# Linear attention in a perceiver block: each key-value and attention product issued as four products of 32 stationary columns on four column positions of TensorE

## The chip, the cores and the metric

The kernel runs on one core of one Trainium2 chip. The metric is the device time of one execution in microseconds (us); lower is better. A change of over 0.5% of it is about what a measurement of this kernel can tell from none.

## What is computed

The reference is one block of a perceiver on x (8 sequences of 64 rows, 512 wide) and a context (8 of 512 rows): cross attention, linear attention, and a mixture of 16 experts with a shared feed-forward, each behind a layernorm and added to x. The change lies in the linear attention alone:

```python
q_proj = _elu1(jnp.einsum('bhnd,hdf->bhnf', q, proj_matrix))   # 16 heads, hd 32, 128 features
k_proj = _elu1(jnp.einsum('bhnd,hdf->bhnf', k, proj_matrix))
kv = jnp.einsum('bhnf,bhnd->bhfd', k_proj, v)
attn = jnp.einsum('bhnf,bhfd->bhnd', q_proj, kv)
k_sum = k_proj.sum(axis=2)
z = 1.0 / (jnp.einsum('bhnf,bhf->bhn', q_proj, k_sum) + 1e-08)
attn = attn * z[..., None]
```

## The kernel before, in words

The 512 tokens (8 sequences of 64) are four tiles of 128 tokens, two sequences in each. Each engine has its own instruction stream, written out by hand, and semaphores tie them together. Cross attention comes first (to about 280 us), then a layernorm, the projection to q, k and v (`qkv_project`, L1127), the linear attention (339 to 388 us), the output product (`residual`, L1093), and the experts.

The order of the linear attention is one list, `LIN_ORDER` (L270 to L282), which PE (TensorE), ACT (ScalarE) and DVE (VectorE) all walk through. Its units are:

- "k" (L1147): the key features of four heads for one token tile, four matmuls with 128 stationary columns and 256 moving ones, in the f32r type. Each is one hardware matmul. ACT takes exp (L560) and for some units relu (L562) of the result, DVE puts them together as `k_feat` (L806, or L810 and L811).
- "q" (L1153): the query features of one head for all 512 tokens, two f32r matmuls with 512 moving columns; ACT and DVE as above (L560, L562, L806).
- "kv" (L1164): for one token tile and four heads, the product of `k_feat` (128 tokens by 128 features, stationary) with `v_bd` (128 tokens by 96 columns, moving: 2 sequences by 48, of which 32 are v and one is ones, for the sum of the features). These are full f32 products, and each is two LDWEIGHTS and two MATMUL records in the trace: 4 heads make 8 records. The result (128 features by 4 x 96 columns) lies in PSUM bank 3 or 4 and is copied to `kv` by ACT (L567, even units) or DVE (L819, odd units). 16 such units.
- "att" (L1176): for one token tile and 8 heads, the product of `q_feat` (128 features by 128 tokens, stationary) with `kv` (128 features by 96, moving), again full f32: 16 records in a unit, two PSUM banks, two sets of banks in turn. DVE adds 1e-8 to the denominators (L828), takes the reciprocal (L831) and multiplies (L834) into `att`. 8 such units; unit a waits until DVE is done with unit a - 2 (`att_done`, L1174).
- "p": four of the projections of q, early in the list.

The list alternates "k" and "kv" 12 times (the "kv" is always the one of four units before), then "q" and "kv" 4 times, then come four "q", then four times two "q" and an "att", and at the end four "att" in a row. After that `att` is transposed (L1185) and copied by ACT (L574) and DVE (L842), and L1093 multiplies by `w_out`.

SyncE starts weight loads at the end of the "kv" units (four loads, L348 to L352) and at the last "att" (the first expert's, L353 on).

Elsewhere the kernel already issues products with fewer than 128 stationary columns. In cross attention L1043 computes the probabilities times v as products with 32 stationary columns, whose results lie on the PSUM partitions 0, 32, 64 and 96 in turn, so that four of them lie side by side in the array, each with 64 moving columns; the four have different moving operands, two by two halves of one tile. Its neighbours in the order of PE are the transposes L1032 (128 stationary columns), the scores L1005 and the projections L959. In the experts L1206 and L1238 have 64 stationary columns on two positions, between products with 128 (L1213, L1227).

Of the kernel before, what the change touches and what calls it, by code (L numbers as in the profile page):

```python
# [20 lines left out]
P = 128  # L21
B, L, S, D = 8, 64, 512, 512
H, HD, FEAT = 16, 32, 128
# [6 lines left out]
HPT = P // HD  # L30
PAIRS = H // 2
SLOTS = B * CAP
KVW = 48
# [5 lines left out]
def perceiver_block(nc, x_d, ctx_d, wq_d, bq_d, wk_d, bk_d, wv_d, bv_d, wo_d, bo_d, wqkv_d, proj_d,  # L39
                    wout_d, bout_d, gate_d, wg_d, wu_d, wd_d, wsg_d, wsu_d, wsd_d, out_d):  # L40
    main = ExitStack()
    with main:
        def sb(stack, name, shape, dt=F32):
            return stack.enter_context(nc.sbuf_tensor(name, shape, dt))
# [73 lines left out]
        k_feat = (k_feat0, k_feat1)  # L118
        v_bd = sb(linear, "v_bd", [P, NT, H, 2, KVW])
# [22 lines left out]
        q_feat = sb(linear, "q_feat", [P, H, TOK])  # L142
# [3 lines left out]
        kv = sb(linear, "kv", [P, NT, H, 2 * KVW])  # L146
# [59 lines left out]
        ps = main.enter_context(nc.psum_tensor("ps", [P, 8, BANK], F32))  # L206

        def bank(n):
            return ps[:, n, :]
# [734 lines left out]
        def _(pe):  # L944
# [122 lines left out]
            for ht in range(KT):  # L1067
                cols = slice(P * ht, P * (ht + 1))
                for dt in range(KT):
                    for i, (w, c) in enumerate(((wq_hi, xn_hi), (wq_hi, xn_lo_cross), (wq_lo, xn_hi))):  # L1070
                        ins = pe.matmul(bank(2 + ht), w[:, dt, cols], c[:, dt, :],  # L1071
                                        start=(dt == 0 and i == 0), stop=(dt == KT - 1 and i == 2))
# [30 lines left out]
            def qkv_out(n):  # L1103
                if "act" in QKV_BY[n]:
                    pe.wait_ge(qkv_act, qkv_count(n, "act"))
                if "dve" in QKV_BY[n]:
                    pe.wait_ge(qkv_dve, qkv_count(n, "dve"))

            def qkv_project(n):
                if 4 <= n < 8:  # L1110
                    qkv_out(n - 4)
                if n < 4:
                    pe.wait_ge(qkv_lo_dve, n + 1)
                else:
                    pe.wait_ge(qkv_lo_pool, 4 if n < 8 else n - 3)
                w_part = wqkv_hi, wqkv_lo
                xn_part = xn_hi, xn_lo
                for dt in range(KT):
                    if n == 0:
                        pe.wait_ge(xn_split, KT + dt + 1)  # L1120
                    for i, (wi, xi) in enumerate(((0, 0), (0, 1), (1, 0))):
                        if 4 <= n < 8:
                            a = xn_part[xi][:, dt, P * (n - 4):P * (n - 3)]
                            c = w_part[wi][:, dt, 2 * D:3 * D]
                        else:
                            a, c = w_part[wi][:, dt, qkv_cols(n)[1]], xn_part[xi][:, dt, :]
                        ins = pe.matmul(bank(qkv_bank(n)), a, c, start=(dt == 0 and i == 0), stop=(dt == KT - 1 and i == 2))  # L1127
                ins.then_inc(qkv_ps, 1)
# [4 lines left out]
            u = w = a = 0  # L1133
            for kind, i, r in LIN_ORDER:
                if kind == "p":
                    qkv_project(i)
                elif kind in "kq":
                    if u == 0:
                        pe.wait_ge(proj_split, 2)
                    if u < 3 or (kind, r) == ("q", 0):  # L1140
                        qkv_out(4 + u if u < 3 else 8 + i)
                    if u >= 3:
                        pe.wait_ge(feat_done, u - 2)
                    if kind == "k":
                        for pr in range(2):
                            for part in range(2):
                                ins = pe.matmul(ps[:, u % 3, 2 * FEAT * pr:2 * FEAT * (pr + 1)],  # L1147
                                                kl_halves[:, i, pr, P * r:P * (r + 1)],
                                                proj_parts[part][:, 2 * i + pr].rearrange("p h f -> p (h f)"),
                                                start=(part == 0), stop=(part == 1))  # L1150
                    else:
                        for part in range(2):
                            ins = pe.matmul(bank(u % 3), proj_parts[part][:, 2 * i + r // 2, r % 2, :],  # L1153
                                            ql_halves[:, i, r // 2, :], start=(part == 0), stop=(part == 1))
                    ins.then_inc(feat_ps, 1)
                    u += 1
                elif kind == "kv":
                    pe.wait_ge(feat_done, 4 * i + r + 1)
                    if w >= 2:
                        pe.wait_ge(kv_done[w % 2], w // 2)  # L1160
                    else:
                        qkv_out(7 + w)
                    for hh in range(HPT):
                        ins = pe.matmul(ps[:, 3 + w % 2, 2 * KVW * hh:2 * KVW * (hh + 1)],  # L1164
                                        k_feat[i % 2][:, r, FEAT * hh:FEAT * (hh + 1)],
                                        v_bd[:, r, HPT * i + hh].rearrange("p u c -> p (u c)"), start=True, stop=True)
                    ins.then_inc(kv_ps, 1)
                    w += 1
                else:
                    for done in kv_done:  # L1170
                        pe.wait_ge(done, NT * KT // 2)
                    pe.wait_ge(feat_done, 16 + 8 * (i + 1))
                    if a >= 2:
                        pe.wait_ge(att_done, a - 1)  # L1174
                    for h in range(2 * HPT):
                        ins = pe.matmul(ps[:, 3 + 2 * (a % 2) + h // HPT, 2 * KVW * (h % HPT):2 * KVW * (h % HPT + 1)],  # L1176
                                        q_feat[:, 8 * i + h, P * r:P * (r + 1)], kv[:, r, 8 * i + h, :],
                                        start=True, stop=True)
                    ins.then_inc(att_ps, 1)
                    a += 1  # L1180
            pe.wait_ge(feat_done, 32)
            for t in range(NT):
                pe.wait_ge(att_done, NT + t + 1)
                for dt in range(KT):
                    ins = pe.transpose(ps[:, ATT_BANK[dt], P * t:P * (t + 1)], att[:, t, P * dt:P * (dt + 1)], ident[:])  # L1185
# [65 lines left out]
            for t in range(NT):  # L1251
                for dt in range(KT):
                    ins = pe.matmul(ps[:, 6, LGW * t:LGW * (t + 1)], xn_T[:, dt, P * t:P * (t + 1)], gate[:, dt, :],
                                    start=(dt == 0), stop=(dt == KT - 1))
# [3 lines left out]
            for t in range(NT):  # L1258
                ins = pe.transpose(ps[0:E, 7, P * t:P * (t + 1)], logit[:, t, :], ident[:])
# [15 lines left out]
            for g in range(2 * KT):  # L1275
                if g >= 2:
                    pe.wait_ge(slot_done, g - 1)
                for i in range(2):
                    t = 2 * (g % 2) + i
                    ins = pe.matmul(ps[:, 5 + 2 * (g % 2), 256 * i:256 * (i + 1)], xn_moe[:, t, P * (g // 2):P * (g // 2 + 1)],  # L1280
                                    pick[:, :, 2 * CAP * t:2 * CAP * (t + 1)], start=True, stop=True)
# [8 lines left out]
            for b in range(B):  # L1290
                ins = pe.transpose(ps[:, 5 + 2 * (b // 4), P * (b % 4):P * (b % 4 + 1)],
                                   pick_w[:, b].rearrange("p e c -> p (e c)"), ident[:])
# [3 lines left out]
            for t in range(NT):  # L1296
                ins = pe.transpose(ps[:, 4, P * t:P * (t + 1)], give_last_T[:, t].rearrange("p h s -> p (h s)"), ident[:])
# [70 lines left out]
```

## Time and profile before

| | us |
|---|---|
| median of 3 runs | 715.52 |
| lowest, highest | 713.46, 716.24 |
| the profiled execution's own time | 715.17 |
| its span in the profile | 713.4 |

The profile is of one execution. PE is TensorE's matmuls, PEld its weight loads, which run beside them. A record's duration holds latency as well; how densely records follow one another is read from their starts, or from a block of x records: its busy time less one record's duration, over x - 1. All rows are of core 0, with times from the start of the span.

### The profile page before, as it was taken

How to read it: one execution, taken by the hardware profiler on the slowest of the kernel's cores; microseconds unless marked ns; L12 is line 12 of the kernel's file. 1: busy time of each engine (PE TensorE's matmuls, PEld its weight loads, DVE VectorE, ACT ScalarE, POOL GpSimd, SP SyncE). 2: the span in 40 equal slices, each digit the busy share in tenths (PEclk: the TensorE clock that was granted, in tenths of full speed). 3: DMA queues.
4: the chain of work that ended last, by engine and by line, in shares of the span. 5: the costliest groups of instructions: out<-in, count | busy, mean ns of one | idle time of the engine just before them, and what ended most of it. 6: DMA issues, size and time to landing. Idle time of an engine off the chain costs nothing.

```text
span 713.4 us, 10423 instructions
## 1 busy us (share of the span) xinstructions
PE 671.5 (94%) x4272; PEld 428.6 (60%) x4272; DVE 290.1 (41%) x595; ACT 240.4 (34%) x468; POOL 42.5 (6%) x43
## 2 busy tenths in 40 slices
PE   6699999999999999699998889999999999999996
PEld 5477777787877776378977474444444444444532
DVE  5844645446264354865776752111111111111212
ACT  5355535445454443355782112111111111111110
POOL 1800000000000000462000100000000000000000
PEclk9999999999999999899999999999999999999999
DMA  8111010110600000303066903799999999999921
GB/s 314 55 59 60 2 61 16 45 60 2 271 24 2 1 1 2 103 1 129 1 266 277 401 1 119 277 411 371 410 360 410 363 393 350 378 391 375 379 72 61
DMA packets 14348, 129.69 MB, mean 182 GB/s; under 512 B 2720, under 2 KB 2848, under 8 KB 6240
## 3 DMA queue, kind: packets, MB, share of 16 engines
q1 hardware_dynamic: 12384, 127.09, 45.9%
q10 hardware_dynamic: 1920, 1.97, 0.9%
q8 instruction: 34, 0.56, 0.3%
q14 instruction: 10, 0.08, 0.0%
HBM read 126.03 MB, written 1.05 MB: 178 GB/s over the span
## 4 chain that ended last, share of the span: by engine, by line
PE 82%; DVE 10%; ACT 4%; issue 1%; DMA 1%; SPq 1%; ACTq 1%; DVEq 0%
PE ps L959 23%; PE ps L1206 15%; PE ps L1238 8%; PE ps L1213 7%; PE ps L1245 4%; PE ps L1127 4%; PE ps L1032 4%; PE ps L1005 2%; PE ps L1043 2%; PE ps L1227 2%; PE ps L1164 2%; PE ps L1071 2%; PE ps L1176 1%; DVE stats L642 1%; PE ps L1093 1%
## 5 line engine op out<-in xcount | busy, mean ns | idle before, releaser
L855 DVE TENSOR_TENSOR hid<-hid,ps 128x256 f32<-128x256 f32 (+1 forms) x32 | 17.6, 554 | 141.6 <-PE ps L1206 91.4
L585 ACT ACTIVATE hid<-ps 128x256 f32<-128x256 f32 (+1 forms) x32 | 15.7, 491 | 141.6 <-PE ps L1213 86.5
L1238 PE MATMUL ps<-w_d,hid_T 128*64 128x512 f32 x256 | 58.4, 598 | 1.3 <-ACT hid_T L600 1.3
L1206 PE MATMUL ps<-w_u,x_slot 128*64 128x512 f32 x256 | 58.4, 598 | 0.0
L1206 PE MATMUL ps<-w_g,x_slot 128*64 128x512 f32 x256 | 57.8, 593 | 0.0
L476 ACT ACTIVATE probs<-ps,neg_max 128x512 f32<-128x512 f32 x64 | 43.6, 688 | 36.2 <-DVE neg_max L723 36.2
L959 PE MATMUL ps<-wv_hi,ctx_hi 128*128 128x512 f32 x128 | 52.5, 410 | 2.7 <-POOL wv_lo L395 2.7
L959 PE MATMUL ps<-wv_lo,ctx_hi 128*128 128x512 f32 x128 | 50.8, 397 | 0.0
L959 PE MATMUL ps<-wv_hi,ctx_lo 128*128 128x512 f32 x128 | 50.4, 394 | 0.0
L702 DVE COPY probs_T<-ps 128x512 f32<-128x512 f32 x32 | 22.1, 692 | 68.7 <-PE ps L1032 68.7
L723 DVE TENSOR_REDUCE neg_max<-ps 128x1 f32<-128x512 f32 x64 | 39.8, 684 | 20.2 <-PE ps L1005 20.2
L959 PE MATMUL ps<-ctx_hi,wk_hi 128*128 128x512 f32 x112 | 44.4, 397 | 0.4 <-ACT k_T L458 0.4
L959 PE MATMUL ps<-ctx_lo,wk_hi 128*128 128x512 f32 x112 | 43.6, 390 | 0.0
L959 PE MATMUL ps<-ctx_hi,wk_lo 128*128 128x512 f32 x112 | 43.6, 390 | 0.0
L1206 PEld LDWEIGHTS ps<-w_g,x_slot 128*64 128x64 f32 x256 | 18.1, 137 | 37.1 <-issue 37.1
L458 ACT ACTIVATE k_T<-ps,bias_k 128x512 f32<-128x512 f32 x32 | 21.7, 690 | 48.8 <-PE ps L959 48.8
L1238 PEld LDWEIGHTS ps<-w_d,hid_T 128*64 128x64 f32 x256 | 17.0, 136 | 34.1 <-issue 32.3
L959 PEld LDWEIGHTS ps<-wv_hi,ctx_hi 128*128 128x128 f32 x128 | 24.3, 190 | 20.1 <-issue 6.5
L1206 PEld LDWEIGHTS ps<-w_u,x_slot 128*64 128x64 f32 x256 | 17.1, 136 | 30.5 <-issue 30.5
L871 DVE TENSOR_TENSOR eo<-ps,eo 64x512 f32<-64x512 f32 x15 | 10.3, 688 | 56.4 <-ACT eo L612 56.4
L612 ACT COPY eo<-ps 64x512 f32<-64x512 f32 x15 | 8.7, 580 | 72.4 <-PE ps L1238 72.4
L715 DVE TENSOR_SCALAR probs<-probs,row_inv 128x512 f32<-128x512 f32 x64 | 31.2, 487 | 2.3
(192 smaller groups left out, 1158.3 us busy)
## 6 DMA issues: line engine op xcount, KB each, us to landing
w_u<-in_wu SPq DMA_DIRECT2D x16, 2048.0 KB, 16.1
w_d<-in_wd SPq DMA_DIRECT2D x16, 2048.0 KB, 14.3
w_g<-in_wg SPq DMA_DIRECT2D x16, 2048.0 KB, 10.2
ctx_raw<-in_ctx SPq DMA_DIRECT2D x7, 1024.0 KB, 4.8
w_qkv<-in_wqkv SPq DMA_DIRECT2D x1, 3072.0 KB, 15.1
ws_g<-in_wsg SPq DMA_DIRECT2D x1, 2048.0 KB, 7.7
ws_u<-in_wsu SPq DMA_DIRECT2D x1, 2048.0 KB, 7.9
ws_d<-in_wsd SPq DMA_DIRECT2D x1, 2048.0 KB, 21.9
```

Source lines behind the costliest of these rows:

```text
L458: act.activation(k_T[:, ht, :], bank(FIRST_K + ht if first else PROJ[ht % 2]), ACT.Identity, bias=bias_k[:, ht:ht + 1], scale=1.0).then_in ...
L476: act.activation(probs[:, p, :], bank(SCORE[p]), ACT.Exp, bias=neg_max[:, p:p + 1], scale=1.0, accum_out=row_sum[:, p:p + 1]).then_inc(exp ...
L702: dve.tensor_copy(probs_T[:, ht % 2, 1].rearrange("p s c -> p (s c)"), bank(TRANS[ht % 2][1])).then_inc(pT_done[1], 1)
L715: dve.tensor_scalar(probs[:, p, :], probs[:, p, :], row_inv[:, p:p + 1], None, ALU.mult).then_inc(prob_done, 1)
L723: dve.tensor_reduce(neg_max[:, p:p + 1], bank(SCORE[p]), AX.X, ALU.max, negate=True).then_inc(max_done, 1)
L959: ins = pe.matmul(dst, a(dt), c(dt), start=(dt == 0 and i == 0), stop=(dt == KT - 1 and i == 2))
L1032: ins = pe.transpose(ps[:, TRANS[ht % 2][pr], P * st:P * (st + 1)], probs[:, 2 * ht + pr, P * st:P * (st + 1)], ident[:])
L1127: ins = pe.matmul(bank(qkv_bank(n)), a, c, start=(dt == 0 and i == 0), stop=(dt == KT - 1 and i == 2))
L1206: ins = pe.matmul(ps[64 * fh:64 * (fh + 1), dst, :], x_slot[:, dt, e, :], weights[e % 2][:, dt, BANK * fh:BANK * (fh + 1)], start=(dt == 0 ...
L1213: ins = pe.matmul(ps[:, dst, 0:w], xn_T[:, dt, P * t:P * (t + 1)], shared[:, dt, f:f + w], start=(dt == 0), stop=(dt == KT - 1))
L1238: ins = pe.matmul(ps[64 * fh:64 * (fh + 1), 6 + n % 2, :], hid_T[:, n % 2, j, 64 * fh:64 * (fh + 1)], w_d[e % 2][:, KT * fh + j, :], start ...
L1245: ins = pe.matmul(bank(6 + n % 2), hid_T[:, n % 2, j, :], ws_d[:, ITEMS[n][2] // P + j, :], start=(j == 0), stop=(j == tiles - 1))
```

## The change

The "kv" and the "att" product of a head, until now with 128 stationary columns, become four products each with 32 of these columns and the same moving operand. Each writes its own 32 partitions of the same PSUM region, at partition 0, 32, 64 or 96. The semaphore is raised by the last of all, as before. Nothing else is changed: no wait, no buffer, no order of the units.

```diff
@@ kv
                     for hh in range(HPT):
-                        ins = pe.matmul(ps[:, 3 + w % 2, 2 * KVW * hh:2 * KVW * (hh + 1)],
-                                        k_feat[i % 2][:, r, FEAT * hh:FEAT * (hh + 1)],
-                                        v_bd[:, r, HPT * i + hh].rearrange("p u c -> p (u c)"), start=True, stop=True)
+                        for c in range(HPT):
+                            ins = pe.matmul(ps[HD * c:HD * (c + 1), 3 + w % 2, 2 * KVW * hh:2 * KVW * (hh + 1)],
+                                            k_feat[i % 2][:, r, FEAT * hh + HD * c:FEAT * hh + HD * (c + 1)],
+                                            v_bd[:, r, HPT * i + hh].rearrange("p u c -> p (u c)"), start=True, stop=True)
                     ins.then_inc(kv_ps, 1)
@@ att
                     for h in range(2 * HPT):
-                        ins = pe.matmul(ps[:, 3 + 2 * (a % 2) + h // HPT, 2 * KVW * (h % HPT):2 * KVW * (h % HPT + 1)],
-                                        q_feat[:, 8 * i + h, P * r:P * (r + 1)], kv[:, r, 8 * i + h, :],
-                                        start=True, stop=True)
+                        for c in range(HPT):
+                            ins = pe.matmul(ps[HD * c:HD * (c + 1), 3 + 2 * (a % 2) + h // HPT,
+                                               2 * KVW * (h % HPT):2 * KVW * (h % HPT + 1)],
+                                            q_feat[:, 8 * i + h, P * r + HD * c:P * r + HD * (c + 1)], kv[:, r, 8 * i + h, :],
+                                            start=True, stop=True)
                     ins.then_inc(att_ps, 1)
```

## Rows read from the trace of the kernel before

**Rows 1.** The page: the engines' busy time, share and instructions

```profile
PE 671.5 (94%) x4272; PEld 428.6 (60%) x4272; DVE 290.1 (41%) x595; ACT 240.4 (34%) x468; POOL 42.5 (6%) x43
```

**Rows 2.** Busy time by stretch; columns: stretch, length, five engines' busy us, clock, DMA

```profile
339.00:361.60 22.60, 22.17 (x186) 21.44 (x185) 17.40 (x30) 17.41 (x36) 0.00 (x0) 1.00 0.01 2
361.60:387.70 26.10, 23.00 (x167) 19.79 (x165) 20.27 (x54) 12.62 (x25) 0.00 (x0) 1.00 0.78 322
...
403.50:409.10 5.60, 2.08 (x17) 1.61 (x16) 4.47 (x12) 1.67 (x4) 1.85 (x2) 1.00 0.99 424
409.10:414.40 5.30, 5.28 (x33) 5.30 (x34) 0.00 (x0) 0.89 (x1) 0.00 (x0) 0.68 0.02 6
440.00:713.40 273.40, 265.94 (x1169) 117.20 (x1167) 43.16 (x71) 37.03 (x76) 0.00 (x0) 1.00 0.86 333
```

**Rows 3.** The chain of work that ended last, 338 to 392 us, its pieces

```profile
344.31 1.10 PE ps L1164 x8
...
362.36 0.60 ACT exps L560
...
367.33 2.00 PE ps L1176 x16
...
378.78 7.45 PE ps L1176 x64
```

**Rows 4.** PE in order of time, two rounds of "k" and "kv"

```profile
344.31 1.10 PE L1164 MATMUL ps<-v_bd,k_feat 128*128 128x96 f32 x8 [0.43 <-DVE kv L819]
...
345.39 0.28 PE L1147 MATMUL ps<-proj_lo,kl_halves 128*128 128x256 f32 x1
345.51 0.28 PE L1147 MATMUL ps<-proj_hi,kl_halves 128*128 128x256 f32 x1
...
345.75 1.03 PE L1164 MATMUL ps<-v_bd,k_feat 128*128 128x96 f32 x8
...
347.12 1.03 PE L1164 MATMUL ps<-v_bd,k_feat 128*128 128x96 f32 x8
```

**Rows 5.** Weight loads by line and shape: busy us, mean ns of one

```profile
L1164 PEld LDWEIGHTS ps<-v_bd,k_feat 128*128 128x128 f32 x128 | 15.8, 191 | 1.1 <-DVE k_feat L811 0.6 <-issue 0.2
...
L1043 PEld LDWEIGHTS ps<-probs_T,v_s 128*32 128x32 f32 x1024 | 16.0, 109 | 7.5 <-issue 7.5
```

**Rows 6.** PE in order of time around two runs of L1043

```profile
99.08 0.39 PE L959 MATMUL ps<-ctx_lo,wk_hi 128*128 128x512 f32 x1
99.31 0.39 PE L959 MATMUL ps<-ctx_hi,wk_lo 128*128 128x512 f32 x1
99.63 1.10 PE L1043 MATMUL ps<-probs_T,v_s 128*32 128x64 f32 x64
100.66 1.97 PE L1032 MATMUL ps<-ident,probs 128*128 128x128 f32 x16
...
105.13 0.50 PE L959 MATMUL ps<-wv_hi,ctx_hi 128*128 128x512 f32 x1
105.47 0.40 PE L959 MATMUL ps<-wv_lo,ctx_hi 128*128 128x512 f32 x1
```

**Rows 7.** PE in order of time, full f32 products elsewhere, and the end of "att"

```profile
479.87 1.24 PE L1213 MATMUL ps<-ws_u,xn_T 128*128 128x256 f32 x5
481.04 1.94 PE L1238 MATMUL ps<-w_d,hid_T 128*64 128x512 f32 x8
...
378.78 7.43 PE L1176 MATMUL ps<-kv,q_feat 128*128 128x96 f32 x64 [1.29 <-DVE q_feat L806]
386.05 1.47 PE L1185 MATMUL ps<-ident,att 128*128 128x128 f32 x12
```

**Rows 8.** DVE in order of time, the last four "att" units

```profile
380.82 0.34 DVE L828 TENSOR_SCALAR den<-ps 64x8 f32<-64x8 f32 x2 [0.94 <-PE ps L1176]
...
381.43 0.86 DVE L834 TENSOR_TENSOR att<-ps,den_inv 64x256 f32<-64x256 f32 x2
...
386.87 0.86 DVE L834 TENSOR_TENSOR att<-ps,den_inv 64x256 f32<-64x256 f32 x2
```

## The prediction, as it was made before the run

> **What bounds the kernel now.** I read the page first: PE is busy for 94% of the span [rows 1], so any time saved on PE should count unless another engine is waited for just there. The table by stretch shows where that is so. The 16 "kv" units lie in 339 to 361.6 us, where PE is busy 22.17 of 22.60 us; the 8 "att" units lie in 361.6 to 387.7, where PE is busy 23.0 of 26.1 and DVE 20.3 [rows 2]. The chain of waits then says which engine sets the pace. It is held up once by DVE's copy of kv, until 344.31 [rows 4]; from there to 361.6 it is PE alone. From 362.36 it runs mostly through ACT's exp and relu and DVE's `q_feat`, with one "att" unit of PE in it (367.33). From 378.78 it is PE again: 64 records of L1176 [rows 3]. So there are three stretches, and what the change does is worth something different in each.
>
> **What a product costs now.** The last 64 records of L1176 take 7.43 us of busy time [rows 7]; less one record's 0.28, over 63, that is 0.1135 us each, with a slow first one; inside a "kv" unit the same sum over (1.03 - 0.28) / 7 gives 0.107, with a fast first one. The period of a "k" and "kv" pair is cleaner: 347.12 - 345.75 = 1.37 us, of which the three plain L1147 records are 0.12 each [rows 4]. I take 0.1115 for a record of 128 stationary and 96 moving columns: eight of these and four of 0.12 make the 1.37, so that passing from one kind of product to the other costs nothing net today.
>
> Is 0.1115 the streaming or the weight load? Full f32 records with other widths tell: 256 moving columns take (1.24 - 0.38) / 4 = 0.215, 128 take (1.47 - 0.27) / 11 = 0.109 [rows 7]. That is 0.83 ns a column and 2 to 3 ns on top, so 96 columns would stream in 0.083. The weights of 128 columns, whose load takes 191 ns against 109 for 32 columns [rows 5], must hold the rate at 0.1115. This is what the change can remove: 0.0285 us a record at most, over 16 x 8 + 8 x 16 = 256 records 7.3 us.
>
> **What it would cost with four positions.** The near row is L1043, the same form with 64 moving columns: 64 records in 1.10 us of busy time [rows 6], less 0.22, over 63: 14 ns each, 0.056 for four. Streaming 64 columns at 0.83 ns is 0.053. So there the weight loads are hidden, and the four positions run side by side at the streaming rate. With 96 columns I take 0.083 for four records. Bounds: 0.056 x 96/64 = 0.084 on the one side with nothing better in reach, since the columns must stream; on the other the present 0.1115, if the loads of four times 32 columns took turns like one of 128. I take 0.083, as L1043 is the nearer row.
>
> **The switch.** L1043 also shows what it costs to change between full-width and 32-column products. Into it: 99.63 - 99.31 = 0.32 us after a product that otherwise takes 0.23, +0.09; with 64 columns the same, 481.04 against the last L1213's start, 479.87 + 4 x 0.215 = 480.73: 0.31 for 0.215. Within and out of it: 100.66 - 99.63 = 1.03 for 16 x 0.056 = 0.90, +0.13. After it, the first full-width record lasts longer until the next: 105.47 - 105.13 = 0.34 for 0.23, +0.11 [rows 6]. Together 0.33 us each time PE goes to narrow products and back. Only a block of over 0.33 / 0.0285 = 12 records earns that back: a "kv" unit has 8, an "att" unit 16, and the four last "att" units together 64. Bounds for the switch: nothing, if what follows hides it, and 0.66, twice the rows.
>
> Here the Trainium skill has a rule against the change. In the trace, records of L1043 start 14 ns apart on average [rows 6]. The page "TensorE: Matmul & The Clock Gate" (section "Wait — 56ns, not 53.3ns?") says that starts of matmuls are never closer than about 25 ns, however few the columns. By it four narrow records would take 0.100, not 0.083; the trace has four in 0.056, so the sum goes by the trace, and the other value is a rival.
>
> **Part by part.**
> 1. "kv" units, 339 to 361.6 us. The pair becomes 8 x 0.083 + 4 x 0.12 + 0.33 = 1.47 instead of 1.37: +0.10. The first three are hidden, since PE waits 0.43 us for DVE anyway before 344.31 [rows 4], more than 3 x 0.10. That leaves 13 periods, of which the first has no switch in (PE has just waited): 13 x 0.10 - 0.09 = +1.2 us. DVE and ACT are busy 17.4 of 22.6 us here [rows 2], so they follow. The loads that SyncE starts behind the last "kv" move by the same 1.2 us, which their users, over 50 us later, don't see.
> 2. The first "att" unit, 367.33: a gain, 16 x 0.0285 = 0.46, less 0.13 and 0.02 for the way out, -0.3. What is late behind it is ACT's exp of the next "q", so it counts. The next three lie under DVE, whose `q_feat` lets PE go on only at 378.78, after 1.29 us of waiting [rows 7]; they gain nothing.
> 3. The last four "att" units. The first ends 0.46 us earlier. After that DVE binds: it needs from 380.82 to 381.43 + 0.86 for a unit, 1.50 with what lies between, and PE would need 16 x 0.083 = 1.33. Now DVE's units start at 380.82 and the last ends at 387.73 [rows 8], so 6.91; then it would be 4 x 1.50 = 6.0. Together -0.46 - 0.91, about -1.4 us. DVE's 1.50 is what is late next. The way out is hidden: the last transposes wait for DVE.
> 4. Three more MATMUL and LDWEIGHTS pairs for each of 256, 768 pairs on 4272 [rows 1]. I cost them at nothing: in the "kv" stretch the 32 + 4 pairs in 1.47 us are thinner than L1043's 64 in 1.03 [rows 6]. In the last "att" units it is 64 pairs in 1.33 to 1.50 us, four times in a row, where L1043 never has more than 64; if that cover fails, part 3 is lost (below).
> Everything behind it moves as one: the expert stretch is PE's (265.9 of 273.4 us) [rows 2].
>
> The sum: +1.2 - 0.3 - 1.4 = -0.5 us on the profiled execution's 715.17, so 714.7. That execution is 0.35 below the median of the runs, 715.52; on the median it is 715.0. It is no change by the bound of 0.5%, 3.6 us.
>
> **The rivals.**
> - **The split binds itself, and it gets slower.** Place: the four positions in a "kv" unit. L1043's four have different moving operands; here four positions read the same one at once, and no row shows that. If they or their weight loads take turns, four records cost 0.1115 or more. From 0.083 up each "kv" pair costs the more: at 0.1115, 0.33 x 13 - 0.09 = +4.2, +0.15 at 367 and nothing at the end, so +4.4, 719.9. It passes the bound of 0.5% at 0.1075 for four, where the sum is 13 x (8 x 0.0245 + 0.10) - 0.09 + 0.1 - 0.3 = +3.6. Against: 0.056 with four loads in it. Chance 0.09.
> - **A floor per record.** The sum with 0.100 for four: "kv" +0.24 x 13 - 0.09 = +3.0; the middle +0.0; the end 16 x 0.0115 = 0.18 for each of four, -0.7: +2.3, so 717.8, and no change by the bound. The page named above would have it so. Chance 0.06.
> - **The switch is hidden.** Then "kv" gains 8 x 0.0285 = 0.228 in each of 13, -3.0, with -0.5 and -1.4: -4.9, so 710.6, faster. Against it: every passage in rows 6 and 7 pays. Chance 0.05. The opposite, a switch of 0.66, is +4.3 on "kv": 719.3; chance 0.03.
> - **Instructions run short in the last 64 x 4 records.** It takes the 1.4 us of part 3 away: 716.4. Four "att" in a row are more than L1043 ever asks, at a time when DMA is at 0.78 of its share [rows 2]. Chance 0.07.
> - **The clock.** At 409 to 414.4 us the granted clock was 0.68 on average, part at 1.2 GHz, after PE had been busy 2.08 of 5.60 us [rows 2]: some 5.3 x 0.32 = 1.7 us. The change makes PE idler at 380 to 388; a second drop costs 1.7 us, 716.7, or it may shift the present one. Chance 0.04.
> The forecast, PE's small loss on "kv" against its gain on "att", has the remaining 0.66.
>
> **How the numbers follow.** The runs shown lie 713.46 to 716.24 apart by themselves. The range takes the forecast, the floor, the short instructions, the clock and these runs' spread: 712.3 to 718.8; a hidden switch, turns at the positions and a double switch are left out, with 0.17. Faster by over 0.5%: 0.05 for the hidden switch and 0.01 beside it, 0.06. Slower by over 0.5%: 0.09 and 0.03, less what of them stays under the bound, 0.10. Within: 0.84.
>
> **What would show it.** In the profile after, L1164 and L1176 have 512 records each of 128*32. A pair of "k" and "kv" has a period of 1.47 us (1.14 if the switch is hidden, 1.70 with turns). The last L1147 record before a "kv" is followed after 0.21 instead of 0.12. A block of "kv" has a busy time of 8 x 0.083 + 0.22, about 0.9. The last "att" units show DVE without a wait and PE waiting for DVE's `att`; DVE's periods there are 1.50, where now they are (6.91 - 1.48) / 3 = 1.81. The linear attention from its first "kv" to the last `att` is shorter by 0.5 us. I am wrong if a pair's period is 1.37 or less or over 1.6, or if DVE still waits for PE after 382 us.

## The result: slower by 0.45%, where no change was forecast

The changed kernel takes 718.09 us (median of 7 runs, 717.11 to 719.85) against 715.38 (7 runs, 713.46 to 717.03): ratio 1.0045, 95% interval 1.0032 to 1.0059. The time forecast was 715.0, "no change". The median lies in the range of 712.3 to 718.8, and a change of 0.45% is still under the bound of 0.5%, but the interval leaves out 1: the kernel is slower, by 3.2 us on the ratio. The forecast said half a microsecond faster.

The page of the kernel after, PE's line [rows 1] and the queue that carries instructions:

```profile
PE 673.2 (94%) x5040; PEld 423.1 (59%) x5040; DVE 289.7 (40%) x595; ACT 241.2 (34%) x468; POOL 43.0 (6%) x43
...
q8 instruction: 40, 0.66, 0.4%
```

768 more matmul records, as the sum had it. The page of the kernel before has 34 packets and 0.56 MB in that queue: six more packets of instructions for 768 more pairs of LDWEIGHTS and MATMUL, 1536 instructions. That makes some 256 instructions, 128 pairs, in a packet, an estimate from these counts.

PE in order of time, in the "kv" stretch of the kernel after [rows 4]; L1165 is the narrow product:

```profile
344.15 0.28 PE L1147 MATMUL ps<-proj_lo,kl_halves 128*128 128x256 f32 x1
344.36 0.87 PE L1165 MATMUL ps<-v_bd,k_feat 128*32 128x96 f32 x32
345.16 0.39 PE L1147 MATMUL ps<-proj_hi,kl_halves 128*128 128x256 f32 x1
345.38 0.28 PE L1147 MATMUL ps<-proj_lo,kl_halves 128*128 128x256 f32 x1
...
345.82 0.87 PE L1165 MATMUL ps<-v_bd,k_feat 128*32 128x96 f32 x32
```

The pair's period is 345.82 - 344.36 = 1.46 us (forecast 1.47, before 1.37). The way in is 344.36 - 344.15 = 0.21, the first gap after it 0.22 instead of 0.12 for a plain one. The 32 records are busy 0.87 us (forecast: about 0.9). So rate and switch came out as priced. The last "att" units did not [rows 7, 8]. The chain of waits of the kernel after:

```profile
378.20 1.36 PE ps L1178 x55
379.56 1.43 issue
380.99 4.37 PE ps L1178 x126
385.36 0.75 issue
386.11 0.54 PE ps L1178 x12
```

Twice PE stands still and no engine releases it; the chain says only "issue", 1.43 and 0.75 us. A third such stall, of 0.38, ends at 374.02. The record before the first stall is the 55th of its unit, so it falls in the middle of a run of matmuls that has no wait in it. DVE, which was to bind, waits instead; DVE in order of time [rows 8]:

```profile
381.71 0.34 DVE L828 TENSOR_SCALAR den<-ps 64x8 f32<-64x8 f32 x2 [2.27 <-PE ps L1178]
...
384.27 0.34 DVE L828 TENSOR_SCALAR den<-ps 64x8 f32<-64x8 f32 x2 [1.09 <-PE ps L1178]
...
386.67 0.34 DVE L828 TENSOR_SCALAR den<-ps 64x8 f32<-64x8 f32 x2 [0.93 <-PE ps L1178]
```

Busy time by stretch [rows 2], with the granted clock and the DMA share as the third and second column from the end:

```profile
378.00:382.00 4.00, 2.37 (x83) 2.19 (x87) 1.62 (x7) 0.00 (x0) 0.00 (x0) 0.85 1.04 438
382.00:390.00 8.00, 6.96 (x198) 6.37 (x189) 5.23 (x19) 0.00 (x0) 0.00 (x0) 0.86 0.09 35
```

PE was busy 2.37 of 4.00 us at 378 to 382. The granted clock is 0.85 and 0.86 on average: it is 1.2 GHz from 380.8 to 384.2, behind the first stall, and 2.4 GHz again before the second. In the block between them 126 records take 4.37 us, 33 ns each, where L1165 has (0.87 - 0.27) / 31 = 19 ns. This is a further stretch of low clock, as one rival feared it, but it came behind a stall.

I cut the linear attention in three by the starts of PE's records: "kv", from the first "kv" product to the first "q" after the last one; "middle", from there to the first product of the last four "att"; "last four", from there to the first transpose of the last token tile.

| | kv | middle | last four | sum |
|---|---|---|---|---|
| before | 22.0 | 17.2 | 9.0 | 48.2 |
| after | 22.9 | 17.0 | 11.5 | 51.4 |
| difference | +0.9 | -0.2 | +2.5 | +3.2 |
| forecast | +1.2 | -0.3 | -1.4 | -0.5 |

The +3.2 us agrees with the 3.2 of the ratio, and nearly all of the error is in the last of the three parts. The two profiled runs themselves differ by 1.9 us in span, not by 3.2: the changed kernel's came to its first "kv" product at 338.30 us, before's at 339.61, and the change touches nothing ahead of that point. Over all the profiled runs of this document it lies anywhere from 338.25 to 340.75. So single profiles are compared below by their stretches, not by their spans. Behind the last four transposes both runs take 325.6 us.

### The profile page after: what moved, and what is told of

Same layout as the page of the kernel before. It is cut to its first block, busy times and chain, and to the rows that moved or that the text cites. A ratio compares the mean times of both kernels' runs of the same rounds, so it can differ in the third digit from the quotient of the medians.

```text
span 715.3 us, 11959 instructions
## 1 busy us (share of the span) xinstructions
PE 673.2 (94%) x5040; PEld 423.1 (59%) x5040; DVE 289.7 (40%) x595; ACT 241.2 (34%) x468; POOL 43.0 (6%) x43
## 4 chain that ended last, share of the span: by engine, by line
PE 81%; DVE 10%; ACT 4%; issue 2%; DMA 1%; SPq 1%; ACTq 1%; DVEq 0%
PE ps L959 22%; PE ps L1209 15%; PE ps L1241 8%; PE ps L1216 7%; PE ps L1248 4%; PE ps L1127 4%; PE ps L1032 4%; PE ps L1005 2%; PE ps L1043 2%; PE ps L1230 2%; PE ps L1071 2%; PE ps L1178 2%; PE ps L1165 1%; DVE stats L642 1%; DMA x<-in_x 1%
```

## The experiments

Two theories at first. **Supply**: a narrow "att" unit takes in 128 PE instructions (weight loads and matmuls) in 1.3 us, and the next ones are not there yet; this could be plain latency, or contention with the expert weights that SyncE has started at 361. **The rivals**: the switch, the clock, or the narrow form itself. Ratios are to runs of the kernel before on the same chip.

### e1, e2, e3: which part costs

e1 splits "kv" alone, e2 "att" alone, e3 only the last four "att" (the edit of e3, shortened; `i == 1` holds for these four):

```diff
-                    for h in range(2 * HPT):
-                        ins = pe.matmul(ps[:, ...], q_feat[:, 8 * i + h, P * r:P * (r + 1)], ...)
+                    n = HD if i == 1 else P
+                    for h in range(2 * HPT):
+                        for c in range(0, P, n):
+                            ins = pe.matmul(ps[c:c + n, ...], q_feat[:, 8 * i + h, P * r + c:P * r + c + n], ...)
```

> Only the 16 kv units are narrow (4 x 32 columns), att stays full. In the changed kernel the stretch of the kv units took 22.92 us against 22.01 before. Theory 'supply' (the loss of the change is mostly PE running out of instructions in the att units): the kv units alone cost +0.9 us, period of a k and kv pair 1.46 us, the last four att as before (9.0 us from their first matmul to the last transposes) and no stall marked issue; time about +1 us over before. Rival 'the switch is all of it': the time is that of the change, +3 us.

> Only the 8 att units are narrow, kv stays full. Supply: the stretch from the first of the last four att units to the last transposes stays long, 10.5 to 12 us against 9.0 before and 11.5 in the change, with gaps marked issue; +1.5 to +2.5 us over before in all. Rival: if the narrow kv units are what upsets the instruction stream (or the clock) there, the att units run clean: that stretch 7.6 us, time -1.5 us.

> Only the last four att units are narrow; the four before them and kv are full. Supply: a 64-record unit takes in 128 instructions in 1.4 us, and what is buffered ahead covers about two units, so there is at least one gap marked issue of 0.5 to 1.5 us, in the third or fourth unit; stretch 8 to 10.5 us, time within 1.5 us of before. Rival (the dense units before them are what empties the buffer, or the clock drop does it): no gap, stretch 7.6 us, time -1.4 us.

e1: 1.0029 (1.0012 to 1.0046), "kv" 22.9 us, last four 9.0, no stall; its linear stretch is 1.0 us longer, yet the time 2.1 us. That surplus was in no theory (see e10). e2: 1.0040 (1.0025 to 1.0054), last four 11.3 with two stalls; its time is 2.9 us over, above the 1.5 to 2.5 expected. e3, with every dense unit before 378 taken out, is no better, 1.0044 (1.0029 to 1.0060). PE in order of time in e3:

```profile
378.08 2.68 PE L1178 MATMUL ps<-kv,q_feat 128*32 128x96 f32 x118 [1.29 <-DVE q_feat L806]
384.38 4.81 PE L1178 MATMUL ps<-kv,q_feat 128*32 128x96 f32 x138 [3.62 <-issue]
```

After 118 records, short of two units, PE waits 3.62 us. So the narrow "kv" units are not the cause, nor are the "att" units in the middle, and the stall is larger than my expectation's 1.5 us, the time 3.1 us over and not within 1.5: both sizes were misses. The granted clock in e3 was 1.00 from 378.0 to 384.4, the whole stall: a fall of the clock does not cause it.

### e4, e8: take the weight transfers away

```diff
-            sp.wait_ge(kv_ps, NT * KT)
+            sp.wait_ge(att_done, 2 * NT)
             sp.dma_start(ws_u[:], wsu_d).then_inc(wsu_in, 16)
             sp.dma_start(w_u0[:], wu_d[0]).then_inc(wu_in[0], 16)
             sp.dma_start(w_d0[:], wd_d[0]).then_inc(wd_in[0], 16)
             sp.dma_start(ws_d[:], wsd_d).then_inc(wsd_in, 16)
-            sp.wait_ge(att_done, 2 * NT)
```

e4 does this to the changed kernel, e8 to the kernel before.

> The changed kernel, with the four weight loads that SyncE starts behind the last kv unit moved behind the last att unit, so that no weight transfer runs during the att units. The linear stretch alone is to be read: the loads come later for the experts, which may cost there. Theory 'contention' (the instruction fetch queues behind weight packets): the gaps marked issue are gone or under 0.3 us each, and the last four att take 7.6 to 8 us. Rival 'latency' (the fetch of 16 KB is too slow for 128 instructions in 1.4 us even on idle DMA): the gaps of about 1.4 and 0.75 us stay, the stretch is 11 to 11.5 us.

> The kernel before (all products full width) with the four weight loads behind the last kv unit moved behind the last att unit: the control for the run e4. Theory 'contention': full-width att units take few instructions and nothing waits for them, so nothing changes: within 0.3 us of before, last four att 9.0 us. Rival (the loads slow the att units themselves, by SBUF or by DVE): the linear stretch gets shorter here too, and the time is 1 to 2 us under before.

PE in order of time in e4, the last four "att":

```profile
378.62 2.92 PE L1177 MATMUL ps<-kv,q_feat 128*32 128x96 f32 x128 [1.44 <-DVE q_feat L805]
381.82 3.03 PE L1177 MATMUL ps<-kv,q_feat 128*32 128x96 f32 x128 [0.28 <-DVE att L833]
```

And DVE in order of time, the same stretch:

```profile
380.20 0.34 DVE L827 TENSOR_SCALAR den<-ps 64x8 f32<-64x8 f32 x2 [0.34 <-PE ps L1177]
...
381.70 0.34 DVE L827 TENSOR_SCALAR den<-ps 64x8 f32<-64x8 f32 x2
...
384.90 0.34 DVE L827 TENSOR_SCALAR den<-ps 64x8 f32<-64x8 f32 x2
```

No stall; PE waits for DVE's `att` as forecast; DVE's units follow one another after 1.50 to 1.70 us; the last four take 7.8 us (forecast 9.0 - 1.4 = 7.6), the linear stretch 47.5, 0.6 us under before, where the prediction had 0.5. e8 shows that full-width products do not care: last four 9.0, ratio 0.9996 (0.9987 to 1.0004). The same instructions run clean without the weight transfers and stall with them, so the transfers are what turns a dense run into a stop.

```profile
q8 instruction: 1, 0.02, 26.1%
```

26.1% of 16 engines for 0.25 us is one packet that takes 1.04 us. Narrower windows give its start:

| stall | packet begins | stall ends | between |
|---|---|---|---|
| change | 371.72 | 374.02 | 2.30 |
| change | 378.49 | 380.99 | 2.50 |
| change | 383.81 | 386.11 | 2.30 |
| e2 | 378.60 | 380.94 | 2.34 |
| e2 | 383.43 | 385.91 | 2.48 |
| e3 | 381.87 | 384.38 | 2.51 |
| e11 (below, no weight transfers) | 379.90 | 382.44 | 2.54 |

Every stall marked "issue" of 0.29 us or more in these linear stretches ends 2.3 to 2.5 us after a packet of instructions begins. The stalls also come at fixed places in the order of instructions, and not at fixed times. PE in order of time in e2, the last four "att":

```profile
378.16 1.36 PE L1177 MATMUL ps<-kv,q_feat 128*32 128x96 f32 x55 [1.27 <-DVE q_feat L806]
380.94 1.79 PE L1177 MATMUL ps<-kv,q_feat 128*32 128x96 f32 x73 [1.43 <-issue]
383.03 1.35 PE L1177 MATMUL ps<-kv,q_feat 128*32 128x96 f32 x53 [0.30 <-DVE att L834]
385.91 1.84 PE L1177 MATMUL ps<-kv,q_feat 128*32 128x96 f32 x75 [1.53 <-issue]
```

Behind the 55th and the 181st record of 256 in e2 and in the change, and behind the 181st in e11: 126 pairs apart, about one packet. The change's stall at 374.02 lies 3 + 4 + 64 + 55 = 126 pairs ahead of its next one. e3 has 192 pairs fewer than e2 ahead of the last four, one packet and a half, and stalls half a packet further on, behind the 118th.

The weight transfers make the packets late. The packet that begins at 378.49 in the change begins at 374.48 in e4, the same one in the same order of instructions. A packet of the kernel before begins at 381.94, and the same one in e8 at 379.51; that costs full-width products nothing. That is the theory "supply", shown: PE runs out of its own instructions when it takes them in fast and the next packet is late. It also tells why stalls outlast the transfers: the packet for the change's second stall begins at 383.81 and lands at 384.9, where the DMA share is down to 0.09 on average, and in e3 PE stands until 384.38. What holds that packet back until 383.81, 2.8 us after PE has resumed, is not shown.

### e9, e4b: the parts timed without the transfers

e9 has only "att" narrow, e4b is e4 again, timed; both with the loads moved.

> Att units narrow, kv full, the four loads moved behind the last att unit. Contention: kv 22.0 us, middle 16.7, last four 7.8, so the linear stretch is 46.6 against 48.2, 1.6 us under before, and 0.9 under the changed kernel with the loads moved. Rival (narrow kv is free or even helps): no gain over that one.

> The kernel of e4 again (the change, loads moved), timed: 47.5 us of linear stretch as in e4, so 0.6 us under before, and 3.5 to 4 us under the change.

The stretches came out as expected: e9 has 22.0, 16.7, 7.9 us, together 46.6; e4b 23.0, 16.7, 7.9, together 47.6. So narrow "att" is worth 1.6 us and narrow "kv" costs 1.0. The times did not follow: e9 1.0002 (0.9991 to 1.0014), e4b 1.0001 (0.9989 to 1.0013). A gain of 1.6 us in the stretch is gone by the end, and e4b is about 3.1 us under the change by the two ratios, not the 3.5 to 4 expected.

### e5: half as many instructions

The last four "att" in two products of 64 columns, `n = 64 if i == 1 else P`, the loads where they were.

> Only the last four att units are split, in two products of 64 columns, the loads where they were: 64 instructions a unit for 128. If the supply of instructions under the weight loads is the limit, the gaps shrink but need not vanish (0 to 2 us where 32 columns had 3.9 us); if two positions stream at 0.083 for two records, DVE binds at 1.50 a unit and the last four take 7.6 to 7.8 us without a gap, -1.2 us. Rival (gaps come from column tiling as such): a gap as in e3, +3 us.

No stall; last four 8.05 us against 9.0, where e4 with four positions and no transfers has 7.8, and DVE waits 0.2 to 0.5 us here and there. The 7.6 to 7.8 expected was missed by 0.25. With half the instructions and all of the transfers PE is fed. Time: 0.9998 (0.9986 to 1.0009): again a gain in the stretch, 1.0 us, that the time does not show.

### e10: where gains and losses go behind the stretch

The kernel before, with the last transposes done three times over, 0.87 us of plain PE work:

```diff
             for t in range(NT):
                 pe.wait_ge(att_done, NT + t + 1)
+                if t == NT - 1:
+                    for dt in (0, 1, 2, 3) * 2:
+                        pe.transpose(ps[:, ATT_BANK[dt], P * t:P * (t + 1)], att[:, t, P * dt:P * (dt + 1)], ident[:])
```

> The kernel before with the last four transposes of att done three times over, 8 more full-width transposes of 0.109 us, 0.87 us on the path; nothing else. It is to tell why e1 cost 2.1 us with a linear stretch only 0.95 longer, and e9 and e5 gained nothing with one shorter by 1.55 and 0.95. Theory 'clock': the router and first expert products run longer at 1.2 GHz when the stage ahead ends at another moment, whatever moved it; then the time is up by 1.5 to 2.3 us, more than the 0.87, and few or none of its runs have the granted clock 0.990 that 23 of 35 runs of before have. Rival 'narrow products lower the clock': up by 0.9 us, with 0.990 in two of three runs.

1.0025 (1.0015 to 1.0035), 1.8 us for 0.87 us of work, as the theory expected, and none of its 9 runs has the mean granted clock 0.990 that 14 of the 19 runs of before beside it have. The groups of instructions by line tell where, at the router's product (`gate`). The kernel before:

```profile
L1253 PE MATMUL ps<-gate,xn_T 128*128 128x96 f32 x32 | 5.4, 349 | 1.2 <-ACT xn_T L432 1.2
```

The same group in e10:

```profile
L1256 PE MATMUL ps<-gate,xn_T 128*128 128x96 f32 x32 | 7.0, 421 | 1.2 <-ACT xn_T L432 1.2
```

And e10's busy time from 410 to 415 us, the granted clock as the third column from the end:

```profile
410.00:415.00 5.00, 5.00 (x26) 5.00 (x25) 0.00 (x0) 0.00 (x0) 0.00 (x0) 0.50 0.00 0
```

In before the clock was 0.66 over 410 to 415 us, in e10 0.50, 1.2 GHz all the time. The router follows a stretch in which PE is mostly idle [rows 2], and in every profile the clock falls once about there. In before it falls 0.9 us after the router's first record and is back after 3.4 us; in e10 it is low from the router's first record on, for 6.8 us.

All sixteen profiles are of one kind or the other. In before, the change, e4, e6, e7b, e8 and e12 the clock falls 0.5 to 1.2 us after the router's first record, for 3.4 us; a record of the router takes 349 or 350 ns, and from the last four transposes to the end of the span it is 325.6 us. In e1, e2, e3, e4b, e5, e6b, e9, e10 and e11 it falls with that record or before it, for 6.8 us; a record takes 375 to 421 ns, and the rest of the kernel 326.5 to 327.2 us. So e1's surplus is the 1.5 us by which it is 327.1 there, and the gains of e5 and e9 are lost there too.

What decides between the two is open. A shift of the work ahead of the router can do it, as e10 shows with full-width products alone, and so do e1 (+1.0 us), e9 (-1.6) and e5 (-1.0), of whose 6, 11 and 12 runs none has 0.990; with e4b's -0.5 it is 5 of 12 runs, with e8's 0.0 it is 9 of 12. But the size of the shift alone does not tell: e7b (-0.9), e6 and the change (+3.1 and +3.2) are of the first kind. Nor does the time since the start of the span: the router's first record is at 409.12 us in before and at 409.10 in e10. The mean clock is a rough sign besides, since it takes in low stretches elsewhere: e12's profiled run has the short one at the router and yet 0.988, with a low stretch more between 20 and 35 us than before's. The changed kernel's profiled run is of the first kind, so this is not what it lost: its clock was low earlier.

### e6, e6b: the price of the switch

e6 makes one of four heads of each "kv" unit narrow (`n = HD if hh == 1 else P`), e6b all in two products of 64 columns.

> In each kv unit only one of the four heads is narrow (8 of its records of 32 columns), the other three full; att full. Theory 'a fixed switch': every passage to narrow and back costs the same 0.33 us however few narrow products there are, so the pair of k and kv is 1.37 - 2 x 0.0285 + 0.33 = 1.64 us, and the kv stretch 25 to 26 us. Rival 'a price per narrow product': a quarter of the change's +0.09, so 1.39 us and 22.3 us.

> kv units in two products of 64 columns on two positions, att full. If the switch is the same for 64 columns as for 32 and two positions also stream at 0.083 for two records, the pair has 1.46 us as in the change. If instead the longer load of 64 columns shows, it is 1.5 or more; if the switch is cheaper, 1.40.

Both were run once, for the stretch alone. e6, PE in order of time:

```profile
344.83 0.37 PE L1147 MATMUL ps<-proj_hi,kl_halves 128*128 128x256 f32 x1
...
346.45 0.36 PE L1147 MATMUL ps<-proj_hi,kl_halves 128*128 128x256 f32 x1
```

The period is 1.62 us (fixed switch: 1.64; per product: 1.39), and "kv" takes 25.2 us. With two of eight old records made narrow the unit is a quarter of a microsecond dearer: the price is one of passing between widths, not of narrow products. e6b has 1.475, "kv" 23.1: 64 columns switch for about the same.

### e11, e7b, e12: fewer switches

"k" and "kv" units in twos, so that one switch serves two "kv" units:

```diff
-            for r in range(4):
-                LIN_ORDER += [(*ahead, r), (*behind, r)]
+            for r in (0, 2):
+                LIN_ORDER += [(*ahead, r), (*ahead, r + 1), (*behind, r), (*behind, r + 1)]
```

e11 does it to the change with the loads moved, e7b to the kernel before, and e12 is e11 with "att" in products of 64 columns.

> The change with the four loads moved, and with k and kv units in twos (k k kv kv) instead of k kv k kv, which halves the switches. Fixed switch: two pairs take 16 x 0.083 + 8 x 0.12 + 0.33 = 2.62 us against 2.73 before and 2.92 in the change, so the kv stretch is 21.2 to 21.6 us if ACT and DVE keep up, the linear stretch 46.0 us against 48.2. Rival (ACT or DVE bind when two k come together, three banks of PSUM): the kv stretch 22 us or more, with waits for k_feat. The time by the stretch is 2 us under before; by the clock theory part of it is lost again.

> The kernel before with k and kv units in twos and everything full width, loads where they were: the control for e11. If full-width products switch for nothing, the order brings only the wait ahead of the fourth kv unit, so the kv stretch is 21.5 to 22.0 us and the time within 1 us of before; e11's 20.3 is then the narrow products' doing. Rival: 20.3 here too, and narrow products bring nothing in twos either.

> e11 with the att units in two products of 64 columns in place of four of 32, so half the instructions there. Supply: no gap marked issue is left (e11 had one of 0.29), DVE binds the last four att at 1.5 to 1.6 us a unit, the linear stretch is 45.0 to 45.5 us against 48.2 before. By the clock theory, which sees the end of the stage, 3 us earlier is nearly as good a moment as before's and gains more of its 3 us than e11 did: 712.5 to 713.5. Rival: 714.5 as e11.

PE in order of time in e11:

```profile
346.40 1.53 PE L1164 MATMUL ps<-v_bd,k_feat 128*32 128x96 f32 x64
347.86 0.39 PE L1146 MATMUL ps<-proj_hi,kl_halves 128*128 128x256 f32 x1
...
349.00 1.20 PE L1164 MATMUL ps<-v_bd,k_feat 128*32 128x96 f32 x48
```

And in the control e7b:

```profile
344.41 1.92 PE L1164 MATMUL ps<-v_bd,k_feat 128*128 128x96 f32 x16
...
347.15 1.92 PE L1164 MATMUL ps<-v_bd,k_feat 128*128 128x96 f32 x16
```

(The last block of e11 is cut short by the window of the view.) Two pairs take 349.00 - 346.40 = 2.60 us narrow (expected 2.62) and 347.15 - 344.41 = 2.74 full. "kv" is 20.3 us in e11 and 21.3 in e7b (22.0 before), where 21.2 to 21.6 and 21.5 to 22.0 were expected: 0.7 is the order's, 1.0 the narrow products'. So they do gain once a switch serves 16 old records. e11: 0.9992 (0.9980 to 1.0003), with 418 ns at the router and still one stall of 0.29 us. e7b: 1.0029 (1.0007 to 1.0051), though its stretch is 0.9 us shorter, and within 1 us was expected; 5 of its 12 runs took over 719 us with a mean clock of 0.979 or 0.981, which no other kernel showed and which I did not follow up.

e12 is faster than the kernel before by a little, and so than the change: 713.68 us, ratio 0.9982 (0.9970 to 0.9994), linear stretch 20.3, 16.8, 7.8, together 44.9 us, no stall (expected: 45.0 to 45.5, and a time of 712.5 to 713.5). In its profiled run the router has 350 ns, though none of its 12 runs reaches 0.990 on the whole. Of the 3.3 us that the stretch gains, the time keeps 1.3.

## Why the prediction was wrong

**The step that failed** is number 4 of the parts, "I cost them at nothing", and with it the term -1.4 of part 3. It let 768 more pairs of instructions go by at no cost, on the ground that L1043 runs 64 pairs in 1.03 us. L1043 does so with next to no DMA beside it (share 0.00 at 99 to 101 us); the "att" units run under the expert weights, DMA share 0.78 [rows 2]. In place of -1.4 the last four took +2.5 us: PE ran out of instructions twice, for 1.43 and 0.75 us, each time until 2.3 to 2.5 us after a late packet of them had begun. Taken apart with e4 (7.8 us without stalls against 11.5): 2.2 us are the two stalls, the other 1.5 the low clock behind the first and DVE's wait that grows out of both. That the time stayed within the stated range is luck: the upper end, 718.8, comes from the floor's 717.8 and the spread of the runs, and the floor is refuted below. The last sign named for being wrong came true: DVE still waits for PE after 382 us, 1.09 and 0.93.

The rival "instructions run short" had the place and the reason, four units in a row under DMA at 0.78, but its price was only the lost gain, 716.4. It took the shortage as a slower rate that costs what was to be won. It is a stop, 0.3 to 3.6 us long, and a stop can cost more than the products ever took. I gave it 0.07.

**What held.** Four narrow records with 96 columns stream in 0.083 us or slightly less, as taken from L1043: 32 records are busy 0.87 us. The switch is 0.33 us a round: a period of 1.46 for 1.47, and e6 shows that it is fixed. Part 1, the "kv" units, +0.9 for +1.2: from the fourth unit on it was 18.3 us for 17.3, the 1.0 that 12 periods of +0.09 make, less 0.07 by which the last block is shorter (the forecast counted 13 periods), and the first three units, whose wait for DVE was to cover them, even came out 0.1 shorter. Part 2, -0.2 for -0.3, with one stall in it. Part 3's mechanism, that DVE binds at 1.50 us a unit, is right without the transfers: e4's whole stretch is 0.6 us shorter than before's, forecast 0.5.

**The rivals.** That four positions reading one moving operand would take turns is refuted. So is the floor per record: records of L1165 follow one another after 19 ns on average, under the 25 ns below which, by the page "TensorE: Matmul & The Clock Gate" of the Trainium skill, section "Wait — 56ns, not 53.3ns?", two starts of matmuls never come. The trace decides here too: the floor does not hold between column positions. In the sums of both these rivals the first three "kv" units were taken as hidden, though 3 x 0.33 and 3 x 0.24 are more than the 0.43 us of waiting there: 0.6 and 0.3 us too little. "The switch is hidden" is refuted by the same 1.46. The Trainium skill's page "TensorEngine Tiling (Array Packing)" says in "Key Properties" that a change of tiling mode drains the engine; the trace agrees in so far as each passage costs, 0.33 us a round, and e6 shows the price alone; whether that is a drain no run here shows. The clock did fall a further time in the profiled run, for 3.4 us from 380.8, which with DVE's share cost 1.5 us, near the rival's 1.7. That fall is not needed for the loss: in e2 the granted clock was 1.00 from 378 to 390 us, and with stalls of 1.43 and 1.53 the last four still took 11.3.

**What I had not seen at all** is that a microsecond gained or lost ahead of the router does not arrive as one at the end. "Everything behind it moves as one" fails by up to 1.6 us, 325.6 for 327.2 behind the last transposes.

## What to carry to other kernels

Splitting a product by columns takes the weight load off its back (0.083 us for 0.1115 here), but it costs a fixed 0.33 us each time PE changes width and four times the instructions: it needs some 12 full-width records between two changes (0.33 / 0.0285), and two positions of 64 columns gave as much without the transfers (7.8 us in e12 as in e4) with half of the instructions. Before counting on a dense run of small matmuls, look at what DMA does just then, not only at whether PE has run as dense elsewhere, and where PE stops at "issue", look for the packets of the instruction queue. Where a kernel has a stretch at the low clock behind an idle one, compare stretches of the trace as well as times, since 1.6 us was lost or won there here by the moment at which the clock fell.

## What the runs showed of the hardware

- PE can stop for want of instructions in the middle of a run without waits: 0.38, 1.43 and 0.75 us in the change, 3.62 in e3, none in e4 with the transfers gone (one of 0.29 in e11). Each of these stalls ends 2.3 to 2.5 us after a packet of the instruction queue begins, and they lie 126 pairs of LDWEIGHTS and MATMUL apart.
- Weight transfers (DMA share 0.93 at 361 to 378 us in the change, 1.04 at 378 to 382) delay such a packet: one begins at 378.49 us in the change and at 374.48 in e4, another at 381.94 in the kernel before and at 379.51 in e8.
- A passage to narrow products and back costs 0.33 us however many there are (period 1.62 in e6, 1.46 in the change), with 64 columns as with 32 (1.475 in e6b).
- On four column positions records with 32 stationary and 96 moving columns follow one another after 19 ns on average (L1165).
- The router's 32 records take 349 ns each, 5.4 us in all, where the clock is low for 3.4 us from 0.9 us after their start (before), and 421 ns, 7.0 us, where it is low for 6.8 us from their start on (e10).
